# Split operands of a decoder layer stored in interleaved pairs instead of two separate halves

## The reference, cut to what matters

```
proj = layernorm(x) @ in_proj_w.T            # 2048x512 @ 512x18560: gate 8192, x 8192, B 1024, C 1024, dt 128
xBC  = silu(causal_conv4(proj[B, C, x]))     # per channel
y    = chunked state-space product of xBC (64 positions of a sequence at once in the kernel)
g    = y * silu(gate);  g = g * rsqrt(mean(g*g over 1024 channels)) * norm_w
x    = x + g @ out_w.T                       # 2048x8192 @ 8192x512
```

## Time and profile before

| | |
|---|---|
| Median of 3 runs | 2838.85 us (2836.41 to 2839.14) |
| The profiled execution's own time | 2837.76 us |
| Its span, first to last instruction | 2836.0 us |
| TensorE matmul busy | 2796.1 us, 99% |
| VectorE, ScalarE, GpSimd busy | 70%, 52%, 46% |
| Mean granted TensorE clock | 0.998 of 2.4 GHz |

### The profile page before, as it was taken

How to read it: one execution, slowest core, us unless ns; L and a number is a source line. 1 busy time by engine, 2 the same in 40 slices (tenths; PEclk the granted TensorE clock), 3 DMA queues, 4 the chain that set the end, 5 groups by cost and what they waited for, 6 DMA issues and landing times.

```text
span 2836.0 us, 56525 instructions
## 1 busy us (share of the span) xinstructions
PE 2796.1 (99%) x22298; PEld 2275.9 (80%) x22298; DVE 1996.7 (70%) x3182; ACT 1462.5 (52%) x2205; POOL 1315.7 (46%) x840
## 2 busy tenths in 40 slices
PE   6999999999999999999999999999999999999998
PEld 5788888878788888887888888888888888888886
DVE  8777768887667667677676766677766666666667
ACT  5666656655454545445355454454544445453545
POOL 4766767775343433443334443434434344343344
PEclk9999999999999999999999999999999999999999
DMA  7788777878565565565665665555655656556530
GB/s 251 275 297 306 257 268 262 277 257 292 175 198 185 180 197 170 188 200 174 205 199 179 190 195 170 187 183 186 204 185 189 196 172 199 186 178 195 183 134 31
DMA packets 179509, 578.41 MB, mean 204 GB/s; under 512 B 25264, under 2 KB 31920, under 8 KB 171184
## 3 DMA queue, kind: packets, MB, share of 16 engines
q1 hardware_dynamic: 179248, 574.79, 61.7%
HBM read 460.42 MB, written 114.29 MB: 203 GB/s over the span
## 4 chain that ended last, share of the span: by engine, by line
PE 91%; DVE 6%; ACT 1%; issue 1%; DMA 0%; POOL 0%; DVEq 0%; SPq 0%; ACTq 0%; POOLq 0%
PE p_in L476 53%; PE p_out L476 24%; PE p_y L476 9%; PE p_in L566 4%; DVE cv L1444 1%; PE p_y L704 1%; DVE o_ring L1384 0%; DVE t_y L1493 0%; DVE mx L1628 0%; DVE g_f L1505 0%; DVE cum L1406 0%; DVE sc L1615 0%; ACT cv L952 0%; DMA raw_w<-wt 0%; ACT L952 0%
## 5 line engine op out<-in xcount | busy, mean ns | idle before, releaser
L476 PE MATMUL p_in<-xnb,w_ring 128*128 128x512 f32 x6864 | 1672.9, 396 | 1.8 <-DVE cv L1444 0.9
L476 PEld LDWEIGHTS p_in<-xnb,w_ring 128*128 128x128 f32 x6864 | 1260.5, 188 | 262.6 <-issue 2.7
L1444 DVE SCALAR_TENSOR_TENSOR cv<-p_in,cpar,cv 128x504 f32<-128x504 f32 x954 | 700.0, 734 | 458.5 <-ACT cv L952 434.8
L1886 POOL TENSOR_TENSOR g_lo<-g_f,g_hi 128x512 fp32r<-128x512 f32 x256 | 338.8, 1325 | 1188.5 <-ACT g_hi L952 1188.5
L476 PE MATMUL p_out<-o_ring,g_hi 128*128 128x512 f32 x2048 | 639.2, 393 | 1.5 <-POOL g_lo L1886 1.5
L952 ACT ACTIVATE cv<-p_in,cpar 128x512 f32<-128x512 f32 x318 | 246.6, 775 | 627.3 <-PE p_in L476 590.9
L476 PEld LDWEIGHTS p_out<-o_ring,g_hi 128*128 128x128 f32 x2048 | 380.1, 188 | 80.3 <-issue 2.1
L476 PE MATMUL p_out<-o_ring,g_lo 128*128 128x512 f32 x1024 | 400.2, 391 | 0.0
L1481 DVE TENSOR_TENSOR x_tok<-p_in,dts 128x512 f32<-128x512 f32 x256 | 176.6, 690 | 283.2 <-PE p_in L566 281.7
L952 ACT ACTIVATE x_t<-cv 128x512 f32<-128x512 f32 x256 | 160.9, 629 | 313.2 <-DVE t_y L1493 288.8
L1897 POOL TENSOR_TENSOR ss<-ss,g_sq 128x512 f32<-128x512 f32 x190 | 309.9, 1631 | 7.5
(11 more groups left out here) (267 smaller groups left out, 2253.5 us busy)
## 6 DMA issues: line engine op xcount, KB each, us to landing
w_ring<-ws_scr SPq DMA_DIRECT2D x432, 512.0 KB, 3.7
o_ring<-ows_scr SPq DMA_DIRECT2D x192, 512.0 KB, 4.6
ws_scr<-w_ring SPq DMA_DIRECT2D x144, 512.0 KB, 6.2
decay<-cum_scr SPq DMA_DIRECT2D x126, 512.0 KB, 6.6
raw_w<-wt SPq DMA_DIRECT2D x144, 256.0 KB, 5.3
ows_scr<-o_ring SPq DMA_DIRECT2D x64, 512.0 KB, 6.4
raw_o<-owt SPq DMA_DIRECT2D x64, 256.5 KB, 5.7
acb<-x SPq DMA_DIRECT2D x3, 1024.0 KB, 7.0
```

Of the source, the lines that this page charges most:

```text
L476: return nc.tensor.matmul(o, lhsT=l, rhs=r, start=first, stop=last)
L1444: ins = V.scalar_tensor_tensor(acc[:, :, t:SEQ], src[:, :, 0:SEQ - t], cpar[:, 5 * m + 3 - t:5 * m + 4 - t], acc[:, :, t:SEQ], ALU.mult, A ...
L1886: T(g_lo[:, c % 2, :], g_f[:, c % 2, :], g_hi[:, c % 2, :].bitcast(F32), ALU.subtract).then_inc(glo_done, 1)
```

## The change

The high part and the remainder of one element now lie beside each other. `w_ring` is [slot, 512 elements, 2] instead of [slot, 2, 4, 128], and `g_hi` and `g_lo` become one tensor `g_hl` of [2, 512, 2]. A stationary operand is now read with a step of two elements (8 bytes); ScalarE writes high parts with that step, and GpSimd reads them and writes the remainders with that step. WS holds the new order, its transfers have the same size. `xnb`, `o_ring`, the moving operands and `wd` keep their form. By the list of allocations `xnb[1]` now starts 128 bytes behind a multiple of 2048 (`st6` and `mv` lie ahead of it), and what follows it up to `g_f` is moved by 128 bytes; `o_ring` is at a multiple of 2048 as before; `g_hl` starts 64 bytes behind the end of `o_ring`, at 64 modulo 2048 (`dpar` and `als` lie between); `wd` is now at 896 modulo 2048.

```diff
-        w_ring = sb("w_ring", [P, RING_W, 2, KT, P], F32R, align=2048)
+        w_ring = sb("w_ring", [P, RING_W, KT * P, 2], F32R, align=2048)
...
-        xnb = [sb(f"xnb{b}", [P, 2, KT, TB], F32R, align=2048) for b in range(2)]
+        xnb = [sb("xnb0", [P, 2, KT, TB], F32R, align=2048)]
+        st6 = sb("st6", [P, QT, 6])
+        mv = sb("mv", [P, QT, 2])
+        xnb.append(sb("xnb1", [P, 2, KT, TB], F32R))
...
-        g_hi = sb("g_hi", [P, 2, TB], F32R, align=2048)
-        g_lo = sb("g_lo", [P, 2, TB], F32R, align=2048)
+        dpar = sb("dpar", [P, CPG])
+        als = sb("als", [P, 1])
+        g_hl = sb("g_hl", [P, 2, TB, 2], F32R)
...
-                        ins = mm(in_bank(k, n), w_ring[:, k % RING_W, w, kt, :], xnb[tb % 2][:, a, kt, :], j == 0, j == 3 * KT - 1)
+                        ins = mm(in_bank(k, n), w_ring[:, k % RING_W, kt * P:(kt + 1) * P, w], xnb[tb % 2][:, a, kt, :], j == 0, j == 3 * KT - 1)
...
-                    for j, (ga, wo) in enumerate(((g_hi, 0), (g_hi, 1), (g_lo, 0))):
-                        ins = mm(p_out[h][:, :], ga[:, c % 2, tok], o_ring[:, c % RING_O, wo, :], c == 0 and j == 0, c == CPG - 1 and j == 2)
+                    for j, (ga, wo) in enumerate(((0, 0), (0, 1), (1, 0))):
+                        ins = mm(p_out[h][:, :], g_hl[:, c % 2, tok, ga], o_ring[:, c % RING_O, wo, :], c == 0 and j == 0, c == CPG - 1 and j == 2)
...
-                copy(w_ring[:, k % RING_W, 0, :, :].rearrange("p k c -> p (k c)"), raw_w[:, slot, :]).then_inc(whi_done, 1)
+                copy(w_ring[:, k % RING_W, :, 0], raw_w[:, slot, :]).then_inc(whi_done, 1)
...
-                copy(g_hi[:, c % 2, :], g_f[:, c % 2, :]).then_inc(ghi_done, 1)
+                copy(g_hl[:, c % 2, :, 0], g_f[:, c % 2, :]).then_inc(ghi_done, 1)
...
-                T(w_ring[:, k % RING_W, 1, :, :].rearrange("p k c -> p (k c)"), raw_w[:, (UNITS * g + k) % RAW_W, :],
-                  w_ring[:, k % RING_W, 0, :, :].rearrange("p k c -> p (k c)").bitcast(F32), ALU.subtract).then_inc(wlo_done, 1)
+                T(w_ring[:, k % RING_W, :, 1], raw_w[:, (UNITS * g + k) % RAW_W, :],
+                  w_ring[:, k % RING_W, :, 0].bitcast(F32), ALU.subtract).then_inc(wlo_done, 1)
...
-                T(g_lo[:, c % 2, :], g_f[:, c % 2, :], g_hi[:, c % 2, :].bitcast(F32), ALU.subtract).then_inc(glo_done, 1)
+                T(g_hl[:, c % 2, :, 1], g_f[:, c % 2, :], g_hl[:, c % 2, :, 0].bitcast(F32), ALU.subtract).then_inc(glo_done, 1)
```

More of the change, by code:

```diff
@@ L70, in decoder_kernel @@
         cpar = sb("cpar", [P, 5 * CONVS])
-        dpar = sb("dpar", [P, CPG])
         dts = sb("dts", [P, QT, HPG])
@@ L74, in decoder_kernel @@
         rms = sb("rms", [P, QT])
-        st6 = sb("st6", [P, QT, 6])
-        mv = sb("mv", [P, QT, 2])
         ve = sb("ve", [P, QT])
@@ L80, in decoder_kernel @@
         dtbs = sb("dtbs", [P, 1])
-        als = sb("als", [P, 1])
         nega = sb("nega", [P, 3])
@@ L297, in store_weights @@
             def store_weights(g, k):
-                sp.dma_start(WS[g, k], w_ring[:, k % RING_W, :, :, :].rearrange("p a k c -> p (a k c)").bitcast(F32)) \
+                sp.dma_start(WS[g, k], w_ring[:, k % RING_W, :, :].rearrange("p c a -> p (c a)").bitcast(F32)) \
                     .then_inc(w_st[k % RING_W], 16)
@@ L305, in load_weights @@
             def load_weights(g, k):
-                sp.dma_start(w_ring[:, k % RING_W, :, :, :].rearrange("p a k c -> p (a k c)").bitcast(F32), WS[g, k]) \
+                sp.dma_start(w_ring[:, k % RING_W, :, :].rearrange("p c a -> p (c a)").bitcast(F32), WS[g, k]) \
                     .then_inc(w_ld[k % RING_W], 16)
@@ L889, in _ @@
                 tok = slice(h * P, (h + 1) * P)
-                for j, (ga, wo) in enumerate(((g_hi, 0), (g_hi, 1), (g_lo, 0))):
-                    ins = mm(p_out[h][:, :], ga[:, c % 2, tok], o_ring[:, c % RING_O, wo, :], False, j == 2)
+                for j, (ga, wo) in enumerate(((0, 0), (0, 1), (1, 0))):
+                    ins = mm(p_out[h][:, :], g_hl[:, c % 2, tok, ga], o_ring[:, c % RING_O, wo, :], False, j == 2)
                 ins.then_inc(part_done, 1)
```

## The result

The changed kernel takes 2872.3 us in the median of 4 runs (2871.2 to 2874.9) against 2838.6 us: a ratio of 1.012, 95% interval 1.0105 to 1.0135, 33.7 us slower where 105 us faster was forecast.

The account below looks back on a forecast made before the run. The prediction took TensorE's matmul pace as the bound. Its terms, -100 - 8 + 3 = -105 us, gave 2734 us (-3.7%); the likeliest case alone spans 2695 to 2790, and for 8 in 10 the range runs to 2880.

Parts of the forecast that it names:

- What bounds the kernel: TensorE: the pace of 9984 matmuls of 128x512, 0.2267 us each, makes 2263 us, 80% of the span.
- The address matters: Matmul pace depends on the address of the next weights: `wd` lasts 397 ns, w_ring 389, since two reads meet in memory.
- Part 1: Stationary reads: an 8-byte step matches the moving stream's speed, saving 10 of 13.3 ns on 9984 matmuls, -100 us.
- Part 2: Units behind a small group: 384 lose 0.03 us each until the streams settle; 8 of 12 us taken as gone.
- Part 3: Splits on ScalarE and GpSimd: +0.1 us each, hidden; 3 us added for first weights and a few late ones.
- Part 4: Transfers and addresses: transfers still have room; moving `xnb[1]` by 128 bytes taken as 0, up to 23 us either way.
- The second: All 9984 matmuls: the stepped load meets the moving stream more often, +6.6 ns each, +66 us, 2905; chance 0.16.
- The first: All weight changes: the 13.3 ns are a fixed price whatever the layout, time 2842; chance 0.14.
- The loads at half speed: Stepped weight loads take some 300 instead of 188 ns, 0.11 us more on 384 bare loads, +42 us, 2881; chance 0.05.
- The control: `wd`, whose form stays, was to keep about 397 ns in the changed profile while the units' matmuls fell to 374 to 380.
- The range: Whole kernel: likeliest case 2695 to 2790 us; for 8 in 10 up to 2880, covering the fixed price and milder slowdowns.

Follow-up runs that it names:

- sweep: Matmuls alone, layer left out, varying stationary step and moving-row address: step 4 bytes took 226.6 ns at phase 0, 233.4 at 8; step 8 took 233.3 at 0.
- addresses-only: Changed kernel's addresses, but high parts and remainders in separate halves with a step of 4 bytes: 2865.0 us, ratio 1.009 to the kernel before.
- shift by 96: Kernel before, step of 4 bytes throughout, only w_ring and g_hi, g_lo moved by 96 bytes: 2890.7 us, ratio 1.0177.
- the map: Matmuls alone again, varying both operands' addresses, stationary step and columns: best 226.6 ns with a step of 4 bytes, 229.9 with 8, for 512 columns.
- units only: Kernel before with only w_ring interleaved, everything at its old address: 2871.9 us, ratio 1.0115.
- the aligned kernel: Changed kernel with xnb[1] and g_hl put back to multiples of 2048 bytes: 2887.2 us, ratio 1.017 to the kernel before.

## Why the prediction was wrong

- **What bounds the kernel**: right. The pace of 9984 matmuls sets the time, and every run moved with it.
- **The address matters**: right, and shown four ways (sweep, addresses-only, shift by 96, and `wd` within the changed kernel). That the two reads meet in the memory is the prediction's reading of it and stays argued. The reading of `wd` against w_ring was the right one. By the list of allocations `wd` lies at a difference of 64 from its moving row (832 modulo 256), where the map has 233 ns, and it took 233.3. The Trainium skill's sentence that the load takes no read bandwidth from the running matmul (TensorE: Matmul & The Clock Gate, what happens when you issue a matmul) doesn't agree with 226.6 against 233.4 ns in the sweep, where only addresses differ.
- **Part 1, the step that failed.** I took the 13.3 ns over 512 / 2.4 as something the two walks do to each other, and let equal speeds remove 10 of them. If it were so, the stepped block would have come near 216 ns at some phase. The runs show a floor of 226.6 ns for 512 columns that no phase and no step went under (229.9 at best with a step of 8 bytes), 229.6 with half the load at the same phase, and 13.7 ns at 384 columns too. So the 13.3 ns were there in every pair of a 128x512 matmul and a full load that was tried, and what addresses and step govern comes on top, from 0 to about 7 ns. What the 13.3 ns consist of stays open. I had the row `wd` for a slower neighbour and none for a faster one, and still took the whole surplus as removable. Instead of -100 us, the step costs 6.6 ns at difference 0 (passes 0 and 2), 4.8 at 128 (passes 1 and 3) and 3.3 at 64 (output product): 3456 x 6.6 + 3456 x 4.8 + 3072 x 3.3 = 50 us.
- **Part 2** took 8 us as gained because the streams would settle at once. Nothing was gained. In the trace of before, the second to eleventh distances in 381 units behind a small group have a mean of 229.7 ns, against 226.7 right behind another unit. With the step (units only) they are 233.2 and 233.7, and without the step but shifted by 96 bytes 234.0 and 234.3: there is no faster pace left to settle into. It does explain the sum. 6912 x 6.7 = 46 us by the steady pace, but the units-only run lost 32.1, 14 less; of these, 381 x 10 x 3.0 ns = 11 us are the matmuls that had already been slower by 3.0 ns. With this, 50 - 14 = 36 against the 33.7 measured; in the changed kernel's trace, from the second iteration on, the distances of the units' matmuls add up to 28 us more than before and those of the output product to 10. The runs' expectations speak of the same 12 or 13 us as settling that is "gone" or "gave back": as a size it held, as a gain it didn't.
- **Part 3**: the splits were hidden, at +42 and +18 ns instead of the +100 taken. The Trainium skill (SBUF — State Buffer, the note on SBUF cachelines) wants two hits on a line of 16 bytes; by this a step of 8 bytes would be free and one of 16 not. The loads took 188, 195 and 310 ns for 4, 8 and 16 bytes, so the cliff at 16 agrees, but 8 bytes cost 7 ns.
- **Part 4**: the moved `xnb[1]` was taken at 0; with the step it gained 1.8 ns in passes 1 and 3 over the aligned place, and `g_hl` at 64 gained 3.4 ns over 0. Together they were worth some 14 us (47.4 - 33.7). By these figures it would have been 3456 x 1.8 + 3072 x 3.4 = 17.
- **The rivals.** The second named the price, 6.6 ns "as `wd`", and this is what the aligned step costs. Its reason, that a stepped load touches twice the lines, is only argued, and a contiguous block at a difference of 32 to 96 costs as much. In `wd` the 6.6 ns come with a difference of 64 and no step, in the aligned kernel with a difference of 0 and a step; whether the two have one cause is open, so that the rival's figure was right by some luck. The first had the right floor and the wrong rest. The loads at half speed (a length of 300) came only with 16 bytes.
- **The control** was badly chosen: `wd` kept its form but not its relative address. Its median went from 397 to 392, because at 896 it lies at a difference of 0 from `xnb[1]` at 128 (389 ns) and of 128 from `xnb[0]` (394).
- **The range.** 2872 lies inside the range up to 2880, but not by the forecast's mechanism: the upper part of the range was there for the rivals.

What makes up the 6.6 ns and the period of 256 bytes inside the memory stays open; no run looked below the distance of two starts. A version that beats the kernel before wasn't found: the map has no pair under 226.6 ns.

## What to carry to other kernels

Read what a matmul costs from the distance of starts, and before a surplus over columns / clock is booked as a gain, look for one row where it is smaller; a slower neighbour shows only that it can get worse. For float32r operands keep (stationary address - moving address) a multiple of 256 bytes and the block contiguous, as measured here for 128x512; against a shift of 96 bytes the placing alone was worth 52 us of 2839. A layout change moves addresses too, so compare it at its own best addresses and at the old ones.

## What was not expected of the hardware

- The pace of a 128x512 float32r matmul depends on the difference of its two operands' addresses modulo 256: 226.6 to 234 ns, with a few pairs of the map that the difference alone doesn't explain.
- A float32r matmul has a surplus of 13.3 ns over its columns at best, one in bfloat16 2.8 ns; nearly no load (2 columns, at 0 and 8 bytes) makes 128 and 256 columns cheaper (+6.7) and 512 dearer (+18).
- A moving row with a step of 8 bytes takes (476.59 - 465.77) / 24 = 451 ns instead of 227, while a stationary block with that step costs at most 7. A step of 16 bytes makes the load 310 ns and the pace 235 to 240.
